# Linear-attention and gated-FFN kernel: the attention quotient between 32x32 block transpositions on VectorE instead of TensorE transposes

## Chip, cores and metric

The kernel runs on one core of one Trainium2 chip (trn2). The metric is the device time of one execution in microseconds; lower is better. Before the change it is 652.47 us, the median of 3 runs (651.65 to 653.05).

## What is computed

The input x has 16 batches of 512 tokens with 128 channels, fp32. Each batch goes through an attention block with eight heads of 16 channels and no softmax, and then through a gated FFN; both have a residual and a layer norm.

```python
normed = rms_norm(x, gamma)
q = taylor(normed @ w_q * 16 ** -0.5)        # [1, q, q x q * 0.5 ** 0.5]: 1 + 16 + 256 features
k = taylor(normed @ w_k); v = normed @ w_v
kv_state = sum_n k[n] v[n]; k_sum = sum_n k[n]
den = q . k_sum
att = (q . kv_state) / maximum(den, 1e-5)
x1 = layernorm(x + att @ w_out)
h = silu(x1 @ w1 * s1) * (x1 @ w2 * s2)      # 128 -> 512
h = gelu(h @ h1 * s); h = gelu(h @ h2 * s)   # 512 -> 512
out = layernorm(x1 + h @ w3 * s3)            # 512 -> 128
```

## The kernel before, in words

A batch passes four stages (FRONT, MIDDLE, FFN, TAIL), one per step, and four batches are in work at once: step t does the front of batch t, the middle of batch t-1, the FFN of batch t-2 and the tail of batch t-3. There are 19 steps; t = 3 to 15 have all four stages. Steps 0 to 2 and the last ones are written out, the others run in a loop. Every engine has its own `step` with its instructions in a fixed, handwritten order; semaphores join them. Nothing is reordered by a compiler, so an instruction that waits holds up everything behind it on its engine.

Numbers are split into a rounded part (hi) and the rest (lo). A product in the FFN is two matmuls of 512 columns, L421 with hi and L422 with lo.

PSUM has eight banks of 512 fp32 columns. Four form `ring` (attention), four `fps` (FFN). The tables `RING` and `FPS` list in TensorE's order what is written to which bank; `bank_wait` makes a write wait until the last content of its bank has been read. In the table before, bank n % 4 goes to the n-th entry.

The front: `transpose_x` and `project_kv` (L304, four token tiles), `project_q`, the sums of pairs of q (`sums_of_q`, sq0 to sq8, L330 to L334), which ScalarE squares into `phiT` (L619), the products of k on VectorE (L248, `phi_k_main`), and `state` (L337), the key/value state, which ScalarE copies to `st`.

The middle: `transpose_state`, `transpose_rest`, then `apply_main` and `apply_rest` (L369, L378) form numerator and denominator of all heads in two banks, acc0 and acc1. They lie channel by token: 32 partitions a head, of which 16 are the numerator and partition 17 (`DEN`) is the denominator. To divide, tokens must be on the partitions. So ScalarE copies both banks to `numden` (L683, L684), TensorE transposes them in eight pieces (`transpose_numden`, L387), VectorE takes maximum, reciprocal and product (`normalise`, L791, once per bank), TensorE transposes the result back in four pieces (`transpose_att`, L395), ScalarE copies it (L695), and `project_out` (L404) multiplies by w_out. `sum_x1` (L814), statistics and a scaling (L810) give x1, which is transposed for the FFN.

The FFN: layer1 (tiles a0, b0 to a3, b3; `silu` on ScalarE, `gate_mult`, `gate_hi`, `gate_lo` on VectorE), layer2 and layer3 (tiles two0 to two3, three0 to three3; two Gelu activations each on ScalarE, L657 and L658, then `gelu_tile` on VectorE, L876), layer4 (y, copied by `copy_y`, L663). layer3 works through hidden tiles 0, 1, 2 for three0 and three1, and each needs the L876 of its tile. The tail: `transpose_y`, `sum_z` (L830), statistics, scaling, store.

The DMA queue only loads x one step ahead, when the bank "out" of the step has been read, and stores the output.

In step 1 ScalarE also sums the low parts of all weights (`weights_lo_sum`, L636, three times), ahead of the first att copy. VectorE takes the largest of these sums (`largest_lo`, L951), TensorE transposes it (L520) and reads it into a register before step 2.

TensorE's order in a full step, with the parts that the change touches marked by a star: 

```
*transpose_state, *layer1(0), layer1(1), transpose_rest, transpose_x, layer1(2), apply_main,
layer1(3), kv0, apply_rest, transpose_y, kv1, layer2(0; 0-2), *transpose_numden x2,
layer2(1; 0-2), layer2(0; 3), layer2(1; 3), *transpose_att, kv2, layer2(2; 0-2), project_out,
project_q, layer2(2; 3), layer2(3), kv3, layer3(0; 0-2), layer3(1; 0-2), sq0, layer3(0; 3),
layer3(1; 3), sq1, sq8, layer3(2; 0-1), sq2, layer3(2; 2-3), sq3, layer3(3; 0-1), transpose_x1,
sq4, layer3(3; 2-3), layer4(0), sq5, layer4(1), *sq6, *state, layer4(2), sq7, layer4(3)
```

VectorE's order around the change (L897 to L928): gate_mult 3, gate_lo 2, gate_hi 3, gate_lo 3, phi_k_main 0, sum_z, normalise 0 and 1, phi_k_main 1, gelu_tile(0,0), the scaling of z, gelu_tile(0,1), sum_x1, gelu_tile(0,2), q_lo, gelu_tile(0,3).

Of the kernel before, what the change touches and what calls it, by code (L numbers as in the profile page):

```python
# [29 lines left out]
P = 128  # L30
# [12 lines left out]
RING = [(what, stage, n % 4) for n, (what, stage) in enumerate((  # L43
    ("stateT", MIDDLE), ("restT", MIDDLE), ("xT", FRONT), ("kv0", FRONT), ("acc0", MIDDLE),
    ("acc1", MIDDLE), ("kv1", FRONT),
    ("nt0", MIDDLE), ("nt1", MIDDLE), ("attT", MIDDLE), ("kv2", FRONT), ("out", MIDDLE), ("qT", FRONT), ("kv3", FRONT),
    ("sq0", FRONT), ("sq1", FRONT), ("sq8", FRONT), ("sq2", FRONT), ("sq3", FRONT), ("sq4", FRONT), ("sq5", FRONT),
    ("sq6", FRONT), ("state", FRONT), ("sq7", FRONT)))]
# [30 lines left out]
def build(nc, x, w_q, w_kv, w_out, w1t, w2t, h1t, h2t, w3t, scales, consts, sel_d, out):  # L79
# [9 lines left out]
    with ExitStack() as ctx:  # L89
# [59 lines left out]
        numden = wide[:, 0:2 * N].rearrange("p (g n) -> p g n", g=2)  # L149
        att_tok, yT = (wide[:, n * N:(n + 1) * N] for n in (2, 3))  # L150
        att = sb("att", [P, N])
        den = sb("den", [P, 2, NT, 4])
        rden = sb("rden", [P, 2, NT, 4])
# [44 lines left out]
        den_ready, rden_ready = sem("den_ready"), sem("rden_ready")  # L198
# [91 lines left out]
        def _(pe):  # L290
# [96 lines left out]
            def transpose_numden(t, g):  # L387
                pe.wait_ge(ring_free[bank_of(RING, f"acc{g}")], read(RING, t, f"acc{g}"))
                bank_wait(RING, ring_free, t, f"nt{g}")
                for j in range(NT):  # L390
                    mm = nc.tensor.transpose(ring[:, bank_of(RING, f"nt{g}"), j * P:(j + 1) * P],  # L391
                                             numden[:, g, j * P:(j + 1) * P], ident)
                mm.then_inc(ring_full, 1)

            def transpose_att(t):  # L395
                for g in range(2):
                    pe.wait_ge(ring_free[bank_of(RING, f"nt{g}")], read(RING, t, f"nt{g}"))
                bank_wait(RING, ring_free, t, "attT")
                for j in range(NT):
                    mm = nc.tensor.transpose(ring[:, bank_of(RING, "attT"), j * P:(j + 1) * P],  # L400
                                             att_tok[:, j * P:(j + 1) * P], ident)
                mm.then_inc(ring_full, 1)

            def project_out(t):  # L404
                pe.wait_ge(ring_free[bank_of(RING, "attT")], read(RING, t, "attT"))
# [62 lines left out]
            def steps_with(with_lo):  # L468
                def step(t, par, front, middle, ffn, tail):
                    if middle:  # L470
                        transpose_state(t)
                    if ffn:
                        layer1(t, 0, with_lo)
                        layer1(t, 1, with_lo)
# [20 lines left out]
                    if middle:  # L495
                        transpose_numden(t, 0)
                        transpose_numden(t, 1)
                    if ffn:
                        layer2(t, 1, (0, 1, 2), with_lo)
                        layer2(t, 0, (3,), with_lo)  # L500
                        layer2(t, 1, (3,), with_lo)
                    if middle:
                        transpose_att(t)
# [49 lines left out]
                    if front:  # L553
                        sums_of_q(t, 6)
                        state(t)
# [25 lines left out]
        def _(act):  # L581
# [84 lines left out]
            def step(t, par, front, middle, ffn, tail):  # L666
# [27 lines left out]
                if middle:  # L694
                    ring_copy(t, "attT", att[:, :], ring[:, bank_of(RING, "attT"), :])  # L695
# [403 lines left out]
```

## Time and profile before

| | |
|---|---|
| median of 3 runs | 652.47 us |
| profiled execution | 652.38 us |
| its span, first to last instruction | 650.6 us |
| TensorE matmul busy (PE) | 586.3 us, 90% |
| TensorE weight load busy (PEld) | 433.1 us, 67% |
| VectorE busy (DVE) | 470.1 us, 72% |
| ScalarE busy (ACT) | 467.5 us, 72% |
| GpSimd busy (POOL) | 147.8 us, 23% |
| mean granted TensorE clock | 0.976 |

The page gives busy time and waits by engine. Consecutive instructions overlap a little, so a busy sum can exceed the time that passes, and a start-to-start distance says more than a duration. A timeline gives each instruction's start; "idle before" in brackets says how long its engine had nothing to do and which instruction ended that. A line can be that of a helper: all ring copies on ScalarE show as L591.

### The profile page before, as it was taken

To read this page: it belongs to the slowest core of one execution; us is meant where nothing else is said; L and a number is where in the kernel's file an instruction comes from. 1 tells how busy PE (TensorE), PEld (TensorE's weight loads), DVE (VectorE), ACT (ScalarE), POOL (GpSimd) and SP (SyncE) were. 2 spreads that over 40 slices of the span, in tenths; PEclk is the share of its full clock that TensorE was granted. 3 is DMA by queue.
4 is the path that set the end of the run, shared out by engine and by line. 5 is a ranking of instruction groups with operands and counts; after the bars stand their busy time and mean duration, and the time that the engine had idled before them with its cause. 6 is when DMAs were issued, how large, how long until landed. Compare 5 with 4: busy or idle time off the path is not lost.

```text
span 650.6 us, 12112 instructions
## 1 busy us (share of the span) xinstructions
PE 586.3 (90%) x3921; PEld 433.1 (67%) x3921; DVE 470.1 (72%) x1069; ACT 467.5 (72%) x938; POOL 147.8 (23%) x216
## 2 busy tenths in 40 slices
PE   2554799999999999999999999999999999999994
PEld 1324577676858677676858677676858777686763
DVE  3466376977869686977959696986959696886673
ACT  2735569596877879686876969687786959686753
POOL 2551122122213122122113122121213122211000
PEclk9877899999999999999999999999999999999998
DMA  7000000000101010010000010000000000000000
GB/s 257 0 1 17 4 16 1 2 34 1 33 1 32 0 32 0 0 32 0 32 0 32 0 31 1 0 32 0 32 0 32 0 6 26 1 17 2 16 18 16
DMA packets 7367, 12.36 MB, mean 19 GB/s; under 512 B 816, under 2 KB 1840, under 8 KB 7344
## 3 DMA queue, kind: packets, MB, share of 16 engines
q1 hardware_dynamic: 7344, 12.06, 5.9%
q8 instruction: 14, 0.23, 0.2%
q14 instruction: 9, 0.07, 0.0%
HBM read 7.86 MB, written 4.19 MB: 19 GB/s over the span
## 4 chain that ended last, share of the span: by engine, by line
PE 59%; ACT 20%; issue 11%; DVE 3%; POOL 1%; ACTq 0%; POOLq 0%; DVEq 0%
PE fps L421 17%; PE fps L422 17%; ACT phiT L619 5%; ACT hid_hi L657 5%; PE ring L375 5%; PE ring L383 5%; PE ring L309 3%; PE ring L408 2%; ACT fps L658 2%; PE ring L391 2%; ACT restq L622 2%; ACT L641 2%; PE ring L316 1%; PE ring L400 1%; PE fps L464 1%
## 5 line engine op out<-in xcount | busy, mean ns | idle before, releaser
L421 PE MATMUL fps<-hid_hi,w_hi 128*128 128x512 f32 x576 | 229.7, 399 | 2.7 <-DVE hid_lo L876 1.4
L422 PE MATMUL fps<-hid_lo,w_hi 128*128 128x512 f32 x576 | 226.5, 393 | 0.0
L657 ACT ACTIVATE hid_hi<-fps,col 128x512 fp32r<-128x512 f32 x128 | 88.3, 690 | 64.2 <-PE fps L422 63.9
L421 PEld LDWEIGHTS fps<-hid_hi,w_hi 128*128 128x128 f32 x576 | 108.2, 188 | 29.9 <-issue 3.4
L876 DVE TENSOR_TENSOR hid_lo<-fps,hid_hi 128x512 fp32r<-128x512 f32 x128 | 88.1, 689 | 53.1 <-ACT fps L658 52.6
L422 PEld LDWEIGHTS fps<-hid_lo,w_hi 128*128 128x128 f32 x576 | 108.3, 188 | 20.9
L858 DVE SCALAR_TENSOR_TENSOR h<-fps,col,gate_zo 128x512 f32<-128x512 f32 x64 | 47.8, 747 | 75.7 <-ACT gate_zo L648 67.5
L619 ACT ACTIVATE phiT<-ring 128x512 f32<-128x512 f32 x128 | 73.6, 594 | 19.6 <-PE ring L330 19.5
L658 ACT ACTIVATE fps<-fps,col 128x512 f32<-128x512 f32 x128 | 84.5, 660 | 0.0
L248 DVE TENSOR_TENSOR phi_k<-phi_k 128x896 f32<-128x896 f32 x64 | 72.6, 1137 | 4.8 <-ACT v_one L591 4.3
L648 ACT ACTIVATE gate_zo<-fps,col 128x512 f32<-128x512 f32 x64 | 44.1, 689 | 40.2 <-PE fps L422 39.5
L1009 POOL TENSOR_TENSOR k_mid<-phi_k,v_one 128x256 f32<-128x256 f32 x32 | 21.4, 668 | 186.9 <-ACT v_one L591 151.2
L421 PE MATMUL fps<-x1T_hi,w_hi 128*128 128x512 f32 x128 | 55.7, 435 | 0.0
L330 PE MATMUL ring<-qT,sel 128*128 128x512 f32 x128 | 53.4, 429 | 1.0 <-DVE qT L779 0.7
L422 PE MATMUL fps<-x1T_lo,w_hi 128*128 128x512 f32 x128 | 51.2, 400 | 0.0
L868 DVE TENSOR_TENSOR hid_lo<-h,hid_hi 128x512 fp32r<-128x512 f32 x64 | 43.7, 683 | 0.5
L641 ACT ACT_TABLE_LOAD x33 | 42.3, 1283 | 1.3 <-PEq L1090 0.7
L347 PE MATMUL ring<-phi_k,v_one 128*32 128x153 f32 x1024 | 37.1, 296 | 4.5 <-ACT phiT L619 4.4
L1032 POOL TENSOR_TENSOR rstd<-veps,const 128x4 f32<-128x4 f32 x16 | 16.1, 1008 | 104.9 <-DVE veps L828 104.9
L347 PEld LDWEIGHTS ring<-phi_k,v_one 128*32 128x32 f32 x1024 | 31.3, 110 | 12.1 <-issue 9.0
L421 PEld LDWEIGHTS fps<-x1T_hi,w_hi 128*128 128x128 f32 x128 | 24.6, 192 | 17.5 <-issue 12.6
L990 POOL TENSOR_TENSOR rn<-ssc,const 128x4 f32<-128x4 f32 x16 | 16.3, 1021 | 80.7 <-DVE ssc L761 77.8
(111 smaller groups left out, 970.0 us busy)
## 6 DMA issues: line engine op xcount, KB each, us to landing
x_b<-in_x SPq DMA_DIRECT2D x16, 256.0 KB, 2.8
out<-gate_zo SPq DMA_DIRECT2D x16, 256.0 KB, 2.8
h<-in_h SPq DMA_DIRECT2D x1, 1024.0 KB, 8.3
gate_zo<-in_h SPq DMA_DIRECT2D x1, 1024.0 KB, 10.4
wide<-in_w SPq DMA_DIRECT2D x3, 256.0 KB, 4.5
sel_raw<-in_sel SPq DMA_DIRECT2D x1, 384.0 KB, 3.6
w_qkv_raw<-in_w_kv SPq DMA_DIRECT2D x1, 128.0 KB, 2.2
const<-in_consts SPq DMA_DIRECT2D x1, 115.0 KB, 2.3
```

The source lines that it names most:

```text
L248: return eng.tensor_tensor(out, fixed, moved, ALU.mult)
L330: mm = nc.tensor.matmul(ring[:, bank, :], sel[:, (f % 4) * P:(f % 4 + 1) * P], qT[f // 4][:, :], start=True, stop=True)
L347: mm = nc.tensor.matmul(ring[32 * hh:32 * hh + 32, bank, g * FEAT:(g + 1) * FEAT], v_one[:, j, 4 * g + hh, :], phi_k[:, j, 4 * g + hh, 0:F ...
L421: nc.tensor.matmul(fps[:, bank, :], w_hi[:, o:o + P], hi, start=start, stop=False)
L422: mm = nc.tensor.matmul(fps[:, bank, :], w_hi[:, o:o + P], lo, start=False, stop=stop and not with_lo)
L619: op = nc.scalar.activation(phiT[:, f, :], ring[:, bank, :], ACT.Square)
L641: nc.scalar.activation(table_use[:, :], source, function)
L648: nc.scalar.activation(gate[:, m % 2, :], fps[:, bank_of(FPS, f"a{m}"), :], ACT.Silu, scale=s1_c[:, m:m + 1]).then_inc(f_free[bank_of(FPS, ...
L657: nc.scalar.activation(hid[1 - layer][0][:, m, :], fps[:, bank, :], ACT.Gelu, scale=scale)
L658: nc.scalar.activation(fps[:, bank, :], fps[:, bank, :], ACT.Gelu, scale=scale)\
L858: nc.vector.scalar_tensor_tensor(out=h32[:, m, :], in0=fps[:, bank_of(FPS, b), :], scalar=s2_c[:, m:m + 1], in1=gate[:, m % 2, :], op0=ALU ...
L876: nc.vector.tensor_tensor(lo, fps[:, bank, :], hi.bitcast(F32), ALU.subtract)\
```

## The change

The denominator and numerator are no longer brought to token order by TensorE. VectorE's transposition works on each 32x32 block by itself: of a tile of 128 x 512 it transposes the 64 blocks in place. As a head occupies 32 partitions, one such operation out of PSUM puts, within every block, the tokens on the partitions and the 32 channels of a head on the columns. VectorE then takes the maximum, the reciprocal and the product for both banks at once, and a second block transposition turns the packed result back to channel by token. Its channel order differs from before (heads of both banks interleaved), so the rows of w_out are permuted on the host. The semaphore `att_ready` goes straight to `project_out`. The three ring entries nt0, nt1 and attT go, and the table gets new banks written out by hand.

With it come moves: on TensorE layer1(0) ahead of transpose_state and state ahead of sq6; on ScalarE sq3 ahead of x1_hi and the state copy ahead of sq6; on VectorE normalise ahead of sum_z.

```diff
@@ -40,12 +40,11 @@
-RING = [(what, stage, n % 4) for n, (what, stage) in enumerate((
-    ("stateT", MIDDLE), ("restT", MIDDLE), ("xT", FRONT), ("kv0", FRONT), ("acc0", MIDDLE),
-    ("acc1", MIDDLE), ("kv1", FRONT),
-    ("nt0", MIDDLE), ("nt1", MIDDLE), ("attT", MIDDLE), ("kv2", FRONT), ("out", MIDDLE), ("qT", FRONT), ("kv3", FRONT),
-    ("sq0", FRONT), ("sq1", FRONT), ("sq8", FRONT), ("sq2", FRONT), ("sq3", FRONT), ("sq4", FRONT), ("sq5", FRONT),
-    ("sq6", FRONT), ("state", FRONT), ("sq7", FRONT)))]
+RING = (
+    ("stateT", MIDDLE, 0), ("restT", MIDDLE, 1), ("xT", FRONT, 2), ("kv0", FRONT, 3), ("acc0", MIDDLE, 0),
+    ("acc1", MIDDLE, 1), ("kv1", FRONT, 2), ("kv2", FRONT, 3), ("out", MIDDLE, 0), ("qT", FRONT, 1), ("kv3", FRONT, 2),
+    ("sq0", FRONT, 3), ("sq1", FRONT, 0), ("sq8", FRONT, 2), ("sq2", FRONT, 1), ("sq3", FRONT, 3), ("sq4", FRONT, 0),
+    ("sq5", FRONT, 2), ("state", FRONT, 1), ("sq6", FRONT, 3), ("sq7", FRONT, 2))
...
-        numden = wide[:, 0:2 * N].rearrange("p (g n) -> p g n", g=2)
+        num_tok = wide[:, 0:2 * N]
...
@@ -384,25 +384,8 @@
-            def transpose_numden(t, g):
...
-            def transpose_att(t):
...
             def project_out(t):
-                pe.wait_ge(ring_free[bank_of(RING, "attT")], read(RING, t, "attT"))
+                pe.wait_ge(att_ready, t)
                 bank_wait(RING, ring_free, t, "out")
@@ -467,10 +450,11 @@
+                    if ffn:
+                        layer1(t, 0, with_lo)
                     if middle:
                         transpose_state(t)
                     if ffn:
-                        layer1(t, 0, with_lo)
                         layer1(t, 1, with_lo)
@@ -492,15 +476,9 @@
                     if ffn:
                         layer2(t, 0, (0, 1, 2), with_lo)
-                    if middle:
-                        transpose_numden(t, 0)
-                        transpose_numden(t, 1)
-                    if ffn:
                         layer2(t, 1, (0, 1, 2), with_lo)
                         layer2(t, 0, (3,), with_lo)
                         layer2(t, 1, (3,), with_lo)
-                    if middle:
-                        transpose_att(t)
@@ -551,8 +529,8 @@
                     if front:
+                        state(t)
                         sums_of_q(t, 6)
-                        state(t)
@@ -679,9 +657,6 @@
-                if middle:
-                    ring_copy(t, "acc0", numden[:, 0, :], ring[:, bank_of(RING, "acc0"), :])
-                    ring_copy(t, "acc1", numden[:, 1, :], ring[:, bank_of(RING, "acc1"), :])
@@ -691,8 +666,6 @@
-                if middle:
-                    ring_copy(t, "attT", att[:, :], ring[:, bank_of(RING, "attT"), :])
@@ -718,10 +691,12 @@
+                if front:
+                    square_sums(t, 3)
                 if middle:
                     x1_hi(t)
                 if front:
-                    square_sums(t, 3, 4)
+                    square_sums(t, 4)
@@ -729,10 +704,9 @@
-                    square_sums(t, 6)
                     ring_copy(t, "state", st[:, :, :].rearrange("p g f -> p (g f)"),
                               ring[:, bank_of(RING, "state"), 0:2 * FEAT])
-                    square_sums(t, 7)
+                    square_sums(t, 6, 7)
@@ -788,20 +762,24 @@
-            def normalise(t, g):
...
+            def normalise(t):
+
+                for g in range(2):
+                    bank = bank_of(RING, f"acc{g}")
+                    dve.wait_ge(ring_full, written(RING, t, f"acc{g}"))
+                    nc.vector.transpose(num_tok[:, g * N:(g + 1) * N], ring[:, bank, :]).then_inc(ring_free[bank], 1)
+                num = num_tok.rearrange("p (g b e) -> p g b e", g=2, e=32)
+                for g in range(2):
+                    dve.wait_ge(ring_free[bank_of(RING, f"acc{g}")], read(RING, t, f"acc{g}"))
+                nc.vector.tensor_scalar(den[:, :, :], num[:, :, :, DEN], DEN_EPS, None, ALU.max).then_inc(den_ready, 1)
+                dve.wait_ge(den_ready, t)
+                nc.vector.reciprocal(rden[:, :, :], den[:, :, :]).then_inc(rden_ready, 1)
+                dve.wait_ge(rden_ready, t)
+                nc.vector.tensor_tensor(att_tok.rearrange("p (b g e) -> p g b e", g=2, e=DH), num[:, :, :, 0:DH],
+                                        rden[:, :, :].unsqueeze(3).to_broadcast([P, 2, N // 32, DH]), ALU.mult)\
+                    .then_inc(att_tok_ready, 1)
+                dve.wait_ge(att_tok_ready, t)
+                nc.vector.transpose(att[:, :], att_tok).then_inc(att_ready, 1)
@@ -901,13 +879,12 @@
                     phi_k_main(t, 0)
-                if tail:
-                    sum_z(t, 1 - par)
                 if middle:
                     if is_step(t, 1):
                         dve.wait_ge(w_lo_ready[0], 1)
-                    normalise(t, 0)
-                    normalise(t, 1)
+                    normalise(t)
+                if tail:
+                    sum_z(t, 1 - par)
@@ -1067,6 +1044,7 @@
+    data["w_out"] = _np.ascontiguousarray(data["w_out"].reshape(2, 4, DH, 128).transpose(1, 0, 2, 3).reshape(128, 128))
```

## Rows read from the trace of the kernel before

**Rows 1.** The page: busy time of the engines and TensorE's granted clock in 40 slices
```profile
PE 586.3 (90%) x3921; PEld 433.1 (67%) x3921; DVE 470.1 (72%) x1069; ACT 467.5 (72%) x938; POOL 147.8 (23%) x216
...
PEclk9877899999999999999999999999999999999998
```

**Rows 2.** Busy by window, one step: length, PE, PEld, DVE, ACT, POOL, clock, DMA
```profile
331.67:368.52 36.85, 35.75 (x245) 26.65 (x246) 28.63 (x66) 28.50 (x59) 8.53 (x14) 1.00 0.04 14
```

**Rows 3.** The same view, two stretches of that step
```profile
339.02:352.82 13.80, 13.72 (x84) 10.44 (x78) 12.98 (x39) 9.09 (x22) 3.61 (x5) 1.00 0.07 19
356.55:369.45 12.90, 11.88 (x108) 9.29 (x107) 7.31 (x13) 12.83 (x24) 3.21 (x6) 1.00 0.00 0
```

**Rows 4.** Timeline of PE: start us, us, engine, line, operation, [idle before <-releaser]
```profile
353.78 0.39 PE L421 MATMUL fps<-hid_hi,w_hi 128*128 128x512 f32 x1
...
368.52 0.43 PE L357 MATMUL ring<-const,st 128*128 128x128 f32 x2 [0.67 <-ACT st L591]
...
369.75 0.39 PE L421 MATMUL fps<-x1T_hi,w_hi 128*128 128x512 f32 x1
```

**Rows 5.** Timeline of DVE in the same step
```profile
342.35 0.68 DVE L835 TENSOR_TENSOR gate_zo<-x,fps 128x512 f32<-128x512 f32 x1
...
344.54 0.17 DVE L796 TENSOR_SCALAR den<-ring 128x16 f32<-128x16 f32 x1
344.74 0.25 DVE L799 RECIPROCAL rden<-den 128x16 f32<-128x16 f32 x1
...
346.20 1.08 DVE L248 TENSOR_TENSOR phi_k<-phi_k 128x896 f32<-128x896 f32 x1
347.20 0.68 DVE L876 TENSOR_TENSOR hid_lo<-fps,hid_hi 128x512 fp32r<-128x512 f32 x1
347.80 1.11 DVE L810 TENSOR_SCALAR gate_zo<-gate_zo,zmv,zrstd 128x128 f32<-128x128 f32 x4
...
349.70 0.69 DVE L817 TENSOR_TENSOR x1p<-x_b,ring 128x512 f32<-128x512 f32 x1 [0.19 <-PE ring L408]
...
352.13 0.69 DVE L876 TENSOR_TENSOR hid_lo<-fps,hid_hi 128x512 fp32r<-128x512 f32 x1 [0.18 <-ACT fps L658]
```

**Rows 6.** Timeline of ACT, end of the same step
```profile
368.75 0.70 ACT L663 ACTIVATE wide<-fps,col 128x512 f32<-128x512 f32 x1
```

**Rows 7.** Timeline of PE around the transposes that the change removes
```profile
342.98 1.04 PE L391 MATMUL ring<-const,wide 128*128 128x128 f32 x8
343.77 0.47 PE L421 MATMUL fps<-hid_hi,w_hi 128*128 128x512 f32 x1
...
345.92 0.39 PE L422 MATMUL fps<-hid_lo,w_hi 128*128 128x512 f32 x1
...
346.77 0.37 PE L309 MATMUL ring<-w_qkv_hi,xnT_hi 128*128 128x264 f32 x1
```

**Rows 8.** Groups by line: line, engine, operation, xcount | busy us, mean ns | idle before
```profile
L876 DVE TENSOR_TENSOR hid_lo<-fps,hid_hi 128x512 fp32r<-128x512 f32 x128 | 88.1, 689 | 53.1 <-ACT fps L658 52.6
...
L864 DVE CAST hid_hi<-h 128x512 fp32r<-128x512 f32 x64 | 26.9, 420 | 0.6
...
L802 DVE TENSOR_TENSOR wide<-ring,rden 128x256 f32<-128x256 f32 x32 | 13.6, 424 | 1.1
```

**Rows 9.** Waits: engine line <- releaser: us in total, times, longest
```profile
PE ring L347 <- ACT phiT L619: 4.4, 13, 0.4
```

**Rows 10.** Timelines of ACT, PE and DVE in step t = 1
```profile
52.36 0.58 ACT L591 ACTIVATE att<-ring 128x512 f32<-128x512 f32 x1
...
61.46 0.37 PE L520 MATMUL fps<-const,lo_max 128*1 128x128 f32 x1 [4.90 <-DVE lo_max L954]
...
55.10 0.69 DVE L817 TENSOR_TENSOR x1p<-x_b,ring 128x512 f32<-128x512 f32 x1 [5.41 <-PE ring L408]
...
57.38 0.68 DVE L779 TENSOR_TENSOR qT<-ring,qT 64x512 fp32r<-64x512 f32 x1
```

More of the change, by code:

```diff
@@ L148, in build @@
         wide = sb("wide", [P, 4 * N])
-        numden = wide[:, 0:2 * N].rearrange("p (g n) -> p g n", g=2)
+        num_tok = wide[:, 0:2 * N]
         att_tok, yT = (wide[:, n * N:(n + 1) * N] for n in (2, 3))
         att = sb("att", [P, N])
-        den = sb("den", [P, 2, NT, 4])
-        rden = sb("rden", [P, 2, NT, 4])
+        den = sb("den", [P, 2, N // 32])
+        rden = sb("rden", [P, 2, N // 32])
         x1p = sb("x1p", [P, NT, D])
@@ L197, in build @@
         st_rest_ready = sem("st_rest_ready")
-        den_ready, rden_ready = sem("den_ready"), sem("rden_ready")
+        den_ready, rden_ready, att_tok_ready, att_ready = (
+            sem(n) for n in ("den_ready", "rden_ready", "att_tok_ready", "att_ready"))
         mv_ready, veps_ready, rstd_ready, x1_ready = (
@@ L385, in apply_rest @@
                     mm.then_inc(ring_full, 1)
-            def transpose_numden(t, g):
[L388 to L393, printed above, removed]
-            def transpose_att(t):
[L396 to L402, printed above, removed]
             def project_out(t):
-                pe.wait_ge(ring_free[bank_of(RING, "attT")], read(RING, t, "attT"))
+                pe.wait_ge(att_ready, t)
                 bank_wait(RING, ring_free, t, "out")
@@ L789, in q_linear @@
                 nc.vector.tensor_copy(restq[1][64:P, :], ring[64:P, bank, :]).then_inc(ring_free[bank], 1)
-            def normalise(t, g):
-                bank = bank_of(RING, f"nt{g}")
-                nt = ring[:, bank, :].rearrange("p (j h e) -> p j h e", j=NT, h=4)
-                dve.wait_ge(ring_full, written(RING, t, f"nt{g}"))
-                nc.vector.tensor_scalar(den[:, g, :, :], nt[:, :, :, DEN], DEN_EPS, None, ALU.max)\
-                    .then_inc(den_ready, 1)
-                dve.wait_ge(den_ready, 2 * (t - 1) + g + 1)
-                nc.vector.reciprocal(rden[:, g, :, :], den[:, g, :, :]).then_inc(rden_ready, 1)
-                dve.wait_ge(rden_ready, 2 * (t - 1) + g + 1)
-                out = att_tok.rearrange("p (j h e) -> p j h e", j=NT, h=H)[:, :, 4 * g:4 * g + 4, :]
-                nc.vector.tensor_tensor(out, nt[:, :, :, 0:DH],
-                                        rden[:, g, :, :].unsqueeze(3).to_broadcast([P, NT, 4, DH]), ALU.mult)\
-                    .then_inc(ring_free[bank], 1)
+            def normalise(t):
[15 more added lines that the diff above has]
+                nc.vector.transpose(att[:, :], att_tok).then_inc(att_ready, 1)
             def norm_scale(n, sm, mv2, rs, s_mv, s_rs, dst, ready):
```

## The prediction

> **What bounds the kernel now.** I read first the page's busy rows: TensorE is busy 90% of the span at a granted clock of 1.00 (2.4 GHz) in most slices (9 stands for 0.9 or more; it is lower in slices 2 to 5) [rows 1], so an operation taken off it looks like time won. The second view, busy time by window, gives the repeating step: 36.85 us, PE busy 35.75, VectorE 28.63, ScalarE 28.50 [rows 2]. Shares hide where each engine binds, so I went to the timelines. Two more windows of the same view, [rows 3], are the finding: from 339.02 to 352.82 VectorE works 12.98 of 13.80 us, and from 356.55 to 369.45 ScalarE works 12.83 of 12.90. Each has a long stretch with practically no slack, and TensorE, which feeds both and waits on both, closes the loop.
>
> The loop, in the step shown: layer1's a1 (PE, 332.90, one period before the 369.75 of [rows 4]) leads to a3, to silu 3 and to gate_mult 3 (VectorE, 339.02). VectorE runs its queue in order from there to gelu_tile(0,2) at 352.13 [rows 5]. TensorE takes that result in layer3 (its matmul at 353.78 [rows 4]). Then three0 fills, ScalarE starts its solid stretch at 356.55 and ends it with copy_y (368.75 plus 0.70 [rows 6]); y's bank frees a1.
>
> **What goes from TensorE.** Eight numden transposes: the first starts at 342.98, the next product at 343.77, so 0.79 us. Four att transposes: the product ahead starts at 345.92 and needs 0.23, the projection behind starts at 346.77, so 0.62 us, a short wait included. The matmul behind each block has 0.47 and 0.37 us instead of 0.39 and 0.28, 0.08 more each. Sum 1.57 us a step [rows 7]. On ScalarE three copies of 128x512 go, 1.8 us; they lie where it waits for TensorE (its solid stretch begins at 356.55), so I count them at nothing in the repeating step.
>
> **What comes onto VectorE.** Removed: two groups of maximum, reciprocal, multiply, 344.54 to 346.20, so 1.66 us [rows 5]. Added: two transpositions out of PSUM, one maximum, one reciprocal, a multiply of 512 columns, a transposition within SBUF. No row shows a block transposition. Below it I put the cast of 128x512 in SBUF, 0.42 us; above it four 128-column instructions in place of one, 1.11 us [rows 5, 8]. The nearest rows are 512 fp32 columns read from PSUM, 0.689 us [rows 8], and I take 0.69 for all three. Starts of neighbours that do not depend on each other are 0.08 closer than their durations (347.20 plus 0.68, next start 347.80), those behind a semaphore 0.03 apart. So: 0.61 + 0.72 + 0.20 (maximum) + 0.37 (reciprocal: 0.25, 0.08 for twice the columns, and the gap; the 0.08 is what 16 columns cost more here than in the maximum) + 0.72 (multiply, 256 columns take 0.42, 512 in the other rows 0.69) + 0.61 = 3.23 us. Net 1.57 us more for VectorE, within its solid stretch.
>
> The Trainium skill, "VectorE: DVE Perf Modes", section "The three transpose paths", gives a 128x128 bf16 transposition as 311 ns on VectorE and 390 on TensorE, and its "Rules for kernel authors" send a 128x128 transposition to TensorE. No row here tests the 311; with one element a cycle, as "Vector Engine (DVE) Microarchitecture Reference", section 3.8, has it, an estimate for 512 columns is 0.71 us, which would put the total 0.9 us higher. The rule argues against this change, and VectorE's full stretch says why it may be right here.
>
> **Does VectorE hold TensorE back?** The stretch has two waits left, before sum_x1 (349.70, shown as 0.19) and before gelu_tile(0,2) (352.13, shown as 0.18); with the 0.08 by which starts could overlap that is 0.27 + 0.26 us [rows 5]. With att ready at about 345.6 and project_out due at 347.0, TensorE does not wait there. But gelu_tile(0,2) now starts at 352.13 + 1.57 - 0.53 = 353.17 and ends at 353.86, while TensorE, 1.57 earlier, wants it at 352.21. So the matmul at 353.78 moves to 353.91: instead of 1.57 us won, 0.13 lost, and TensorE stands 1.7 us at layer3's third tile (L421), waiting for L876. **The removed TensorE time is turned into a wait on VectorE.**
>
> **Moves and their cover.** layer1(0) goes ahead of transpose_state. Today TensorE waits 0.67 us there for the state copy, 0.85 counting from the spacing of two matmuls [rows 4]. In its place a1 waits for copy_y, whose time is set by ScalarE's solid stretch, in which the same instructions are only reordered. It ends at 369.45; a1 starts 0.13 behind it (as the transposes do behind the state copy), 369.58 instead of 369.75: 0.17 won. state before sq6, and its bank freed by sq2 instead of sq3, removes a wait of 0.35 (4.4 us in 13 waits [rows 9]), but a1 waits for ScalarE all the same, so that is worth nothing. three3 now waits about 0.3 us for its bank (gelu_tile(1,0) starts near 359.5 instead of 358.9); the 1.2 us that just came free cover that. sq7's bank waits for sq5 instead of sq4, ended 366.1, wanted at 366.8. normalise ahead of sum_z delays sum_z by about 3.2 us; behind it are the yT bank, wanted by two3 at 349.1, freed at 346.2; the POOL power and the output's store, which nothing waits for; and phi_k_main(1). The load of x waits for sum_x1, about a microsecond later, and has most of a step. The permuted w_out is made on the host: nothing.
>
> **Sum.** A repeating step changes by 0.13 - 0.17 = -0.04 us; 13 of them (t = 3 to 15) give -0.5. In t = 2 there is no sum_z (342.35 to 344.54, 2.19 us [rows 5]) and no final scale, so VectorE is early and TensorE keeps its gain: -1.57 - 0.17 = -1.7. In t = 16, without front work, the same count gives +0.15.
>
> The first attention step (t = 1) is another matter. There the att copy stands in ScalarE's queue behind the three sums over the weights' low parts and starts at 52.36; project_out follows, then sum_x1 at 55.10, and at 61.46 TensorE waits 4.90 us for lo_max, which VectorE reaches behind all that [rows 10]. Without the copy att is ready at about 48.7 and sum_x1 starts near 50.9. q_lo must then wait for the q copies, which are still behind those sums: 53.1 plus 0.6, so 53.75 instead of 57.38, 3.65 us earlier; the chain behind moves with it. At the end of this step state and sq7 come about 0.4 earlier, and a0 is not behind the state transposes, 0.24. Together -4.3.
>
> -0.5 - 1.7 + 0.15 - 4.3 = -6.4 us. The profiled execution took 652.38 us (span 650.6 and 1.8 around it), the median of the runs is 652.47: forecast **646.0 us**. Each 0.1 us on the price of a transposition is 0.3 a step and, over 14 steps, 4.2 us.
>
> **Rivals.**
> (A) The forecast: both loops bind, 641 to 651 us. Chance 0.66.
> (B) Slower: a transposition costs more than other 512-column instructions, with its place in VectorE's stretch before gelu_tile(0,2). It decides from 6.4 / (3 x 14) = 0.15 over my price, 0.84 us each; at the upper bound of 1.11 it is +17.6, 663.6 us. For it: no row shows the instruction. Against: everything simple with 512 columns out of PSUM takes 0.67 to 0.69. Chance 0.16, a third of it near zero change.
> (C) TensorE stays the bound and the whole gain comes: 15 x (1.57 + 0.17) + 4.3 = 30.4, so 622 us. For it: 90% busy. Against: VectorE's stretch would have to end 1.6 us sooner than its queue adds up to. Chance 0.08.
> (D) The first step's gain does not come, because something else holds lo_max (the third sum ends only at about 52.4, and largest_lo waits for it): 650.3 us. Against: the wait names VectorE, and 57.8 is well behind 52.4. Chance 0.10.
> If the last transposition alone ran at the cast's 0.42 it would be 14 x 0.27 = 3.8 less, 642.2, within (A).
>
> **Numbers.** (A) with its bounds is 641 to 651; down to 638 takes cheap transpositions with a little more slack, up to 655 takes in (D) and (B) to 0.9 us each. Outside are most of (C) and half of (B). A difference of 0.2%, 1.3 us, is what a measurement can tell. Faster: nearly all of (A), (C), half of (D): 0.74. Same: 0.13. Slower: 0.13.
>
> **What would show it.** A period near 36.8 us; PE waits at L421 for L876 (about 1.7 us a step) and for copy_y (0.8), together nearly as large as the time removed; no wait at L357 or L347; VectorE solid from gate_mult 3 to gelu_tile(0,2) with transpositions of 0.69; lo_max's transpose at about 57.8. Wrong if the period is near 35.1 (then C), or over 37.2 with transpositions over 0.84 (B).

## The result, and the profile after

The changed kernel takes 679.58 us (median of 4 runs, 678.40 to 681.73) against 652.06 us for the kernel before beside it: a ratio of 1.042 (95% interval 1.039 to 1.045). It is **slower by 27.5 us**, where 6.4 less was forecast.

The page after, where it answers to [rows 1]: busy times, and TensorE's granted clock in 40 slices.
```profile
span 678.1 us, 11624 instructions
...
PE 588.8 (87%) x3729; PEld 427.5 (63%) x3729; DVE 500.6 (74%) x1069; ACT 440.0 (65%) x890; POOL 158.6 (23%) x216
...
PEclk9876999899998989899898989989898998989898
```
192 TensorE instructions are gone and yet its busy time is 2.5 us longer; the second row says why: in about every second slice the clock is below 9 tenths, where before it was so only in slices 2 to 5 and in the last.

The waits of PE after (releaser: us in total, times, longest):
```profile
PE fps L404 <- DVE hid_lo L854: 34.1, 30, 2.1
...
PE fps L404 <- ACT wide L641: 9.3, 14, 0.9
```
L404 and L405 are the hi and lo products (L421 and L422 before), L854 is gelu_tile (L876), L641 copy_y. These are the two waits that the prediction named, in the places it named; the first is longer.

**Closing the loop.** I cut one period of the prediction's loop at five events and read each from the timelines. After, two kinds of period alternate.

| stretch | before | as predicted | after |
|---|---|---|---|
| gate_mult 3 to gelu_tile(0,2) | 13.11 | 14.15 | 15.18 / 15.21 |
| to TensorE's third tile | 1.65 | 0.74 | 0.74 / 0.74 |
| to ScalarE's gelu(1,0) | 2.77 | 2.77 | 4.01 / 4.31 |
| to the end of copy_y | 12.90 | 12.90 | 12.92 / 12.92 |
| to the next gate_mult 3 | 6.38 | 6.21 | 6.24 / 6.26 |
| period | 36.81 | 36.77 | 39.09 / 39.44 |

Three stretches came out as predicted to within 0.05 us. Two did not: the first is 1.05 too long, the third 1.24 or 1.54. Over the whole trace, counted from transpose_x1 to transpose_x1, the period is 39.28 us in the mean of 13 steps against 36.83.

*The first stretch.* VectorE's timeline, then POOL's, in the step that begins at 346.65 (start us, us, engine, line, [idle before]):
```profile
346.65 0.75 DVE L836 SCALAR_TENSOR_TENSOR h<-fps,col,gate_zo 128x512 f32<-128x512 f32 x1 [0.63 <-ACT gate_zo L626]
...
349.98 1.31 DVE L770 STREAM_TRANSPOSE wide<-ring 128x512 f32<-128x512 f32 x2
351.33 0.70 DVE L774 TENSOR_SCALAR den<-wide 128x32 f32<-128x32 f32 x1
352.06 0.35 DVE L776 RECIPROCAL rden<-den 128x32 f32<-128x32 f32 x1
352.45 0.69 DVE L778 TENSOR_TENSOR wide<-wide,rden 128x512 f32<-128x512 f32 x1
353.17 0.71 DVE L782 STREAM_TRANSPOSE att<-wide 128x512 f32<-128x512 f32 x1
...
355.96 1.09 DVE L248 TENSOR_TENSOR phi_k<-phi_k 128x896 f32<-128x896 f32 x1
356.97 0.69 DVE L854 TENSOR_TENSOR hid_lo<-fps,hid_hi 128x512 fp32r<-128x512 f32 x1
358.06 1.11 DVE L788 TENSOR_SCALAR gate_zo<-gate_zo,zmv,zrstd 128x128 f32<-128x128 f32 x4 [0.40 <-POOL zrstd L1009]
...
361.86 0.69 DVE L854 TENSOR_TENSOR hid_lo<-fps,hid_hi 128x512 fp32r<-128x512 f32 x1
```
```profile
351.22 0.76 POOL L990 TENSOR_TENSOR phi_k<-phi_k,k_mid 128x256 f32<-128x256 f32 x1
356.10 1.82 POOL L1009 TENSOR_TENSOR zrstd<-zveps,const 128x4 f32<-128x4 f32 x1 [4.12 <-DVE zveps L824]
```
The transpositions, the multiply and the reciprocal cost what was taken for them. The maximum of 32 columns does not: it takes 0.70 where 0.20 was taken, and it stands beside GpSimd's L990, ending 0.05 behind it. And the power for zrstd takes 1.82, where the kernel before has 1.01 for it; it starts 0.14 behind L248 on VectorE, a product of two SBUF inputs. The scaling of z (L788) has to wait for it: 0.40 shown, 0.48 by the start it would have had at 0.08 before the end of the L854 ahead. Together 0.53 + 0.48 = 1.01 of the 1.05.

*The third stretch.* TensorE's timeline behind the wait, in that step and then in the one before it:
```profile
359.82 0.50 PE L404 MATMUL fps<-hid_hi,w_hi 128*128 128x512 f32 x1 [0.33 <-DVE hid_lo L854]
...
362.60 0.79 PE L404 MATMUL fps<-hid_hi,w_hi 128*128 128x512 f32 x1 [2.04 <-DVE hid_lo L854]
363.19 0.63 PE L405 MATMUL fps<-hid_lo,w_hi 128*128 128x512 f32 x1
363.62 0.63 PE L404 MATMUL fps<-hid_hi,w_hi 128*128 128x512 f32 x1
...
365.75 0.40 PE L405 MATMUL fps<-hid_lo,w_hi 128*128 128x512 f32 x1
365.99 0.39 PE L330 MATMUL ring<-qT,sel 128*128 128x512 f32 x1
```
```profile
323.48 0.50 PE L404 MATMUL fps<-hid_hi,w_hi 128*128 128x512 f32 x1 [2.05 <-DVE hid_lo L854]
...
324.74 0.58 PE L405 MATMUL fps<-hid_lo,w_hi 128*128 128x512 f32 x1
325.11 0.63 PE L404 MATMUL fps<-hid_hi,w_hi 128*128 128x512 f32 x1
```
Matmuls that start every 0.23 us elsewhere start every 0.43 here: the lower of the two clock levels, 1.2 GHz instead of 2.4. Busy by window says the same (length, PE, PEld, DVE, ACT, POOL, clock):
```profile
358.80:367.00 8.20, 5.83 (x19) 4.06 (x19) 7.92 (x20) 2.74 (x8) 2.80 (x4) 0.79 0.22 64
```
In one kind of period the slow matmuls begin right behind the wait of 2.04 us, in the other 1.3 us later; that is the alternation of 39.4 and 39.1. The wait is twice paid: once as the wait, and once as the speed of what was held up.

**The rest of the span.** transpose_x1 of step 1 starts at 58.80 instead of 64.26. Of these 5.46 us, 1.56 are there when kv0 of step 1 starts (41.59, 43.15 before), and 3.9 come behind it. Of the 1.56, 0.36 lie before TensorE's first matmul (9.86, 10.22 before); the other 1.2 come in steps 0 and 1. One part of them is in step 0, where the kernel before waits for the bank of kv2, and the changed kernel, with its new bank table, doesn't:
```profile
15.13 0.59 PE L309 MATMUL ring<-w_qkv_hi,xnT_hi 128*128 128x264 f32 x1 [0.66 <-ACT v_one L591]
```
How the rest of the 1.2 divides over banks, order and clock is not shown. The next period is 1.34 shorter, but seven matmuls of it ran at the lower clock before and one after, which is most of that. Then 13 periods are 2.45 longer each, the last 2.50: -5.46 - 1.34 + 31.85 + 2.50 = 27.55, the difference of the two spans (678.1 - 650.6) to 0.05.

### The profile page after: what moved, and what is told of

Its sections match the earlier page's. It is cut to its first block, busy times and chain, and to the rows that moved or that the text cites. A ratio compares the mean times of both kernels' runs of the same rounds, so it can differ in the third digit from the quotient of the medians.

```text
span 678.1 us, 11624 instructions
## 1 busy us (share of the span) xinstructions
PE 588.8 (87%) x3729; PEld 427.5 (63%) x3729; DVE 500.6 (74%) x1069; ACT 440.0 (65%) x890; POOL 158.6 (23%) x216
## 4 chain that ended last, share of the span: by engine, by line
PE 29%; DVE 24%; ACT 19%; issue 16%; POOL 5%; DVEq 1%; ACTq 0%; POOLq 0%
PE fps L404 10%; PE fps L405 8%; ACT phiT L597 5%; PE ring L375 5%; POOL zrstd L1009 4%; ACT fps L636 3%; ACT hid_hi L635 3%; DVE hid_lo L854 3%; DVE wide L770 3%; DVE phi_k L248 2%; DVE gate_zo L788 2%; PE ring L330 2%; ACT gate_zo L626 2%; ACT wide L641 2%; DVE zstats L818 2%
## 5 line engine op out<-in xcount | busy, mean ns | idle before, releaser
L404 PE MATMUL fps<-hid_hi,w_hi 128*128 128x512 f32 x576 | 241.7, 420 | 35.4 <-DVE hid_lo L854 34.1
L405 PE MATMUL fps<-hid_lo,w_hi 128*128 128x512 f32 x576 | 238.0, 413 | 0.0
L404 PEld LDWEIGHTS fps<-hid_hi,w_hi 128*128 128x128 f32 x576 | 114.6, 199 | 71.5 <-DVE hid_lo L854 47.4
L405 PEld LDWEIGHTS fps<-hid_lo,w_hi 128*128 128x128 f32 x576 | 115.5, 201 | 23.9
L854 DVE TENSOR_TENSOR hid_lo<-fps,hid_hi 128x512 fp32r<-128x512 f32 x128 | 88.0, 689 | 52.1 <-ACT fps L636 51.1
L248 DVE TENSOR_TENSOR phi_k<-phi_k 128x896 f32<-128x896 f32 x64 | 70.6, 1105 | 5.6 <-ACT v_one L569 5.1
L404 PE MATMUL fps<-x1T_hi,w_hi 128*128 128x512 f32 x128 | 55.2, 432 | 13.7 <-ACT wide L641 9.3
L330 PE MATMUL ring<-qT,sel 128*128 128x512 f32 x128 | 55.9, 448 | 1.9 <-DVE qT L753 0.7
L1009 POOL TENSOR_TENSOR zrstd<-zveps,const 128x4 f32<-128x4 f32 x16 | 26.6, 1663 | 105.8 <-DVE zveps L824 105.8
L569 ACT ACTIVATE phi_k<-ring 128x128 f32<-128x128 f32 (+1 forms) x128 | 24.9, 257 | 39.6 <-PE ring L309 38.5
L405 PE MATMUL fps<-x1T_lo,w_hi 128*128 128x512 f32 x128 | 50.4, 393 | 0.0
L404 PEld LDWEIGHTS fps<-x1T_hi,w_hi 128*128 128x128 f32 x128 | 24.0, 187 | 34.7 <-issue 17.8
L347 PE MATMUL ring<-phi_k,v_one 128*32 128x153 f32 x1024 | 37.2, 298 | 0.0
```

Source lines behind the costliest of these rows:

```text
L248: return eng.tensor_tensor(out, fixed, moved, ALU.mult)
L330: mm = nc.tensor.matmul(ring[:, bank, :], sel[:, (f % 4) * P:(f % 4 + 1) * P], qT[f // 4][:, :], start=True, stop=True)
L404: nc.tensor.matmul(fps[:, bank, :], w_hi[:, o:o + P], hi, start=start, stop=False)
L405: mm = nc.tensor.matmul(fps[:, bank, :], w_hi[:, o:o + P], lo, start=False, stop=stop and not with_lo)
L854: nc.vector.tensor_tensor(lo, fps[:, bank, :], hi.bitcast(F32), ALU.subtract)\
L1009: nc.gpsimd.tensor_tensor(rs[:, :], var[:, :], neg_half[:, :], ALU.pow).then_inc(rs_ready, 1)
```

## The experiments

Three things are suspected, and all would follow from VectorE's queue: the maximum beside GpSimd, the power beside L248, and the clock behind the wait. The rival is that the transposition as such costs too much there. Ratios are to the kernel before on the same chip, with the 95% interval.

**1. Fill the wait, and change nothing else.** Eight more matmuls (`fill`, four products of hi and lo into the bank of three1 before it is wanted) stand between layer3's second and third tile in the full steps.
```diff
-                        layer3(t, 0, (0, 1, 2), with_lo)
+                        layer3(t, 0, (0, 1), with_lo)
+                        if middle and tail:
+                            fill(t, 4, with_lo)
+                        layer3(t, 0, (2,), with_lo)
                         layer3(t, 1, (0, 1, 2), with_lo)
```


> The changed kernel; TensorE repeats one product (8 matmuls of 512 columns, 1.85 us, result overwritten later) in the wait of 2.04 us before layer3's third tile, in the steps with all of middle and tail. Theory (three added costs: the maximum waits for GpSimd, 0.5 us; GpSimd's power is slowed and the scaling of z waits for it, 0.5 us; and TensorE's clock halves behind the 2 us wait, 1.3 us a step): the matmuls behind the wait come every 0.23 us again, not every 0.43, the period falls from 38.97 to about 37.7 and the total from 678 to about 661 us. Rival (the halved clock is hidden behind the wait for the next VectorE result, gelu_tile(0,3), and the loop is VectorE's alone): the clock comes back and the total stays at 677 to 680 us.

661.76 us, 1.013 (1.009 to 1.016), as expected. Periods of 38.04 in the mean, and behind step 2 not one slow matmul (PE, the third tile):
```profile
353.95 0.50 PE L404 MATMUL fps<-hid_hi,w_hi 128*128 128x512 f32 x1 [0.20 <-DVE hid_lo L862]
354.28 0.39 PE L405 MATMUL fps<-hid_lo,w_hi 128*128 128x512 f32 x1
```
**More work on TensorE makes the kernel 18 us faster**: of 39.28 us a period, 1.24 are the clock's, and nothing else was touched.

**2. Take GpSimd away from the maximum.** `k_small(0)` goes behind both powers in POOL's queue.
```diff
-                if front:
-                    k_small(t, 0)
 ...
                     inv_std(t - 1, veps_ready, veps, rstd, rstd_ready)
+                if front:
+                    k_small(t, 0)
```


> The changed kernel with GpSimd's small products of token tiles 0 and 1 (L986 to L990) moved behind its two powers, away from the quotient on VectorE. Theory: the maximum (L774) falls from 0.68 to about 0.2 us in every step, VectorE reaches gelu_tile(0,2) 0.5 us sooner, period 38.5, total about 671 us. Rival (reading 32 columns at a stride of 32 from SBUF is what makes the maximum slow): it stays at 0.68 and so does the total, 678 us. Either way the power of zrstd keeps its 1.8 us.

659.00 us, 1.010 (1.007 to 1.013), 12 better than expected. The maximum takes 0.19:
```profile
L774 DVE TENSOR_SCALAR den<-wide 128x32 f32<-128x32 f32 x16 | 3.1, 192 | 0.8
```
The price of the maximum was right; what came on top is the clock. The wait is as long as before, and what is behind it is not slow (PE):
```profile
351.87 0.40 PE L405 MATMUL fps<-hid_lo,w_hi 128*128 128x512 f32 x1
354.30 0.50 PE L404 MATMUL fps<-hid_hi,w_hi 128*128 128x512 f32 x1 [2.04 <-DVE hid_lo L854]
354.64 0.39 PE L405 MATMUL fps<-hid_lo,w_hi 128*128 128x512 f32 x1
```
So the length of this one wait does not decide it: at 2.04 us the clock falls in every period of the changed kernel and in only one here, where a period is 37.55, 38.04 (experiment 1) less the 0.5. The stretches around it are not equal, though: the changed kernel also waits 0.33 at the tile before (359.82 above), which is gone here, also in the one period that falls.

**3. Give TensorE other work during the wait.**
```diff
-                        layer3(t, 0, (0, 1, 2), with_lo)
-                        layer3(t, 1, (0, 1, 2), with_lo)
+                        layer3(t, 0, (0, 1), with_lo)
+                        layer3(t, 1, (0, 1), with_lo)
+                        layer3(t, 0, (2,), with_lo)
+                        layer3(t, 1, (2,), with_lo)
```


> The changed kernel; on TensorE layer3(1) of tiles 0 and 1 stands ahead of layer3(0) of tile 2, so that 4 useful matmuls (0.93 us) fall into the wait. Theory: the wait shrinks from 2.04 to about 1.1 us and three0 is full when gelu_tile(0,3) allows it, 1.0 to 1.3 us sooner; period 37.7 to 38.0, total 661 to 665 us, a little more if the clock still halves. Rival (VectorE's loop alone): 677 to 680 us.

663.92 us, 1.016 (1.008 to 1.024), as expected; the interval is wide, since its two executions are 4 us apart. The wait is now 1.13 and 0.75 us, the period 38.0 with two of 39.4, in which seven and eight matmuls are slow. Work brought forward keeps the clock like the filler in all but these two, and shortens nothing else: VectorE sets the time.

**4. Take VectorE work out of the stretch: sum_x1 behind gelu_tile(0,3).**
```diff
-                if middle:
-                    sum_x1(t, 1 - par)
                 if ffn:
                     gelu_tile(t, 0, 2)
 ...
                     gelu_tile(t, 0, 3)
+                if middle:
+                    sum_x1(t, 1 - par)
```


> The changed kernel with sum_x1 and its statistics (2.2 us of VectorE) moved behind gelu_tile(0,3), out of the stretch that TensorE waits for. Theory (VectorE's queue before gelu_tile(0,2) is the bound): gelu_tile(0,2) starts 2.2 us sooner, the wait on TensorE all but goes, the clock stays at 1.00, and the next bound is ScalarE's stretch before copy_y: period about 35.5, total 630 to 640 us, faster than both kernels. Rival (the bank that sum_x1 frees is then late for sq1): a new wait of 1 to 2 us at sq1, period 37, total 650 to 655 us.

674.35 us, 1.032 (1.029 to 1.035): a miss by 34 and more. The wait comes back one result later (PE):
```profile
334.00 0.51 PE L404 MATMUL fps<-hid_hi,w_hi 128*128 128x512 f32 x1 [2.08 <-DVE hid_lo L854]
```
Here it is three3 that waits for its bank, which gelu_tile(1,0) frees. VectorE is full beyond gelu_tile(0,2), up to gelu_tile(1,0), and what leaves the first part only goes to the second. (The scaling of x1 was also slower now, 1.72 instead of 1.11, beside GpSimd.) Most periods are 38.0; in three of the thirteen, of 39.5 to 39.8, six to eight matmuls behind this wait are slow. Another 8 us of the miss lie in steps 1 and 2, where transpose_x1 comes 4.2 and then 7.8 us later than in the changed kernel.

**5. As 2, with the scaling of z behind gelu_tile(0,3).** This takes away the wait for the power too.
```diff
-                if tail:
-                    norm_scale(t - 3, z, zmv, zrstd, ...)
 ...
                     gelu_tile(t, 0, 3)
+                if tail:
+                    norm_scale(t - 3, z, zmv, zrstd, ...)
```


> Run e2 (GpSimd's small products moved away) and also the scaling of z moved behind gelu_tile(0,3) on VectorE, so that nothing waits for the slowed power of zrstd and 1.5 us leave the stretch before gelu_tile(0,2). Theory, corrected by e4 (VectorE is in work without a gap from gate_mult 3 to gelu_tile(1,0), and taking work out of its first part only moves TensorE's wait to three3's bank): the wait at layer3's third tile falls from 2.0 to 0.6 us, that at layer3(3) grows from 0.5 to about 1.5; the period gains only the 0.4 us of the removed wait, 37.1, total about 651 us. Rival (only the stretch before gelu_tile(0,2) counts): period 36.0, total about 637 us.

651.20 us, 0.998 (0.997 to 1.000), as expected: period 37.26, no slow matmuls behind step 2, VectorE's wait for zrstd gone. But TensorE still waits 0.62, 0.64 and 1.22 us, and the scaling pays for its new neighbour on GpSimd with 2.21 us instead of 1.11:
```profile
351.85 2.21 DVE L788 TENSOR_SCALAR gate_zo<-gate_zo,zmv,zrstd 128x128 f32<-128x128 f32 x4
```

**6. Relieve VectorE.** As 2, scaling of z behind gelu_tile(0,2); the q copies (1.4 us, `q_linear`) and gate_hi 3 go to ScalarE, the copies behind `copy_q`.
```diff
 (VectorE)
-                    q_linear(t)
-                    gate_hi(t, 3)
 (ScalarE)
                     copy_kv(t, 0)
+                if ffn:
+                    act.wait_ge(f_free[bank_of(FPS, "b3")], read(FPS, t, "b3"))
+                    nc.scalar.activation(hid[0][0][:, 3, :], h32[:, 3, :], ACT.Copy).then_inc(hi_ready, 1)
 ...
                     copy_q(t)
+                    q_linear(t)
```


> e5's idea with less work on VectorE: the scaling of z right behind gelu_tile(0,2), the two copies of q for the linear features (1.4 us) and the cast gate_hi 3 (0.45 us) given to ScalarE, in its idle time. Theory: gelu_tile(1,0) starts 2.2 us sooner than in e2 (37.55 us a period), so that TensorE and ScalarE bound again: period 35.4 to 36.0, clock at 1.00 throughout, total 632 to 641 us, faster than both kernels. Rival (ScalarE, given 1.8 us more, becomes the bound): period 36.8 or more, total over 650 us.

656.16 us, 1.005 (1.004 to 1.007): a miss by 15 and more. 1.8 us less on VectorE, of which the scaling of z, 1.71 instead of 1.11 beside GpSimd, takes back 0.6, and the period is 37.4: TensorE now waits for ScalarE as well (sq0 for q, 0.29; gelu_tile(0,3) behind its activation, 0.87; a1 for copy_y, 0.84). ScalarE is no reserve at this place, and period and total are those of the rival.

**7. The change without its quotient.** The kernel before, with the moves on TensorE and ScalarE only; sum_z stays ahead of normalise, and the bank table is the old one with state and sq6 exchanged.
```diff
-                    if middle:
-                        transpose_state(t)
                     if ffn:
                         layer1(t, 0, with_lo)
+                    if middle:
+                        transpose_state(t)
 ...
-                        sums_of_q(t, 6)
                         state(t)
+                        sums_of_q(t, 6)
```
(and on ScalarE the copy of the state ahead of the squares of 6, the squares of 3 ahead of x1_hi)

> The kernel before with the moves on TensorE and ScalarE alone: layer1(0) ahead of transpose_state, state ahead of sq6 with the bank of sq2, sq3 ahead of x1_hi, state copy ahead of sq6; the quotient as before. Theory: the waits at L357 and L347 (13.6 us in all) go, but ScalarE's stretch before copy_y sets the pace, so only 0.1 to 0.2 us a step are won: total 649 to 651 us. Rival (those waits were time): 13 us less, 639 us.

649.79 us, 0.996 (0.995 to 0.997). Period 36.69 (36.83 before), the waits at L357 and L347 gone, a1 waiting for copy_y (11.9 us in 14). These moves are worth 0.14 us a period (0.17 was taken).

**8. Undo one reordering: sum_z ahead of normalise, as it was.**
```diff
+                if tail:
+                    sum_z(t, 1 - par)
                 if middle:
                     if is_step(t, 1):
                         dve.wait_ge(w_lo_ready[0], 1)
                     normalise(t)
-                if tail:
-                    sum_z(t, 1 - par)
```


> The changed kernel with sum_z ahead of normalise on VectorE, as it was before. Theory: the maximum meets no GpSimd products (0.2 us), the power of zrstd takes 1.0 us and its result is there in time, so 1.0 us leaves VectorE's stretch; att is ready 2 us later and project_out waits about 0.9 us, but that only takes from the wait behind it; the clock falls seldom or never. Period 37.5 to 38.0, total 657 to 663 us. Rival (the quotient has to come first, since project_out holds up all of layer3): 678 us or more.

649.28 us, 0.995 (0.993 to 0.997), 8 better than the lower end of what was expected. **The order of two entries in VectorE's queue is 30 us**, and the period is 37.03, with no slow matmul behind step 2. VectorE and POOL of this kernel:
```profile
339.36 1.31 DVE L770 STREAM_TRANSPOSE wide<-ring 128x512 f32<-128x512 f32 x2
340.71 0.19 DVE L774 TENSOR_SCALAR den<-wide 128x32 f32<-128x32 f32 x1
```
```profile
338.42 0.75 POOL L990 TENSOR_TENSOR phi_k<-phi_k,k_mid 128x256 f32<-128x256 f32 x1
339.50 1.01 POOL L1009 TENSOR_TENSOR zrstd<-zveps,const 128x4 f32<-128x4 f32 x1 [0.33 <-DVE zveps L824]
```
L990 is over when the maximum starts, and the power runs beside the transpositions out of PSUM at its full speed. The three block transpositions themselves are unchanged, so the rival that they are too dear here falls. The waits that are left:
```profile
PE ring L391 <- DVE att L782: 14.4, 15, 2.4
...
PE fps L404 <- DVE hid_lo L854: 8.8, 16, 0.7
PE fps L404 <- ACT wide L641: 8.6, 13, 0.9
```
project_out waits 0.83 a step for att, since the quotient now stands behind sum_z. The repeating step wins nothing by all this: 37.03 us against 36.83 in the kernel before. What is won against that kernel lies in steps 0 and 1: transpose_x1 of step 1 starts at 57.99 instead of 64.26.

**9 and 10. Use VectorE's slack where it is, behind gelu_tile(1,0).** Both are experiment 2 with phi_k_main and the scaling of z moved late. In 9 (norm_scale also leaves its place behind gelu_tile(0,0)):
```diff
                     q_linear(t)
-                    phi_k_main(t, 2)
 ...
                     gelu_tile(t, 1, 0)
                 if front:
-                    phi_k_main(t, 3)
+                    phi_k_main(t, 2)
                 if ffn:
                     gelu_tile(t, 1, 1)
+                if front:
+                    phi_k_main(t, 3)
+                if tail:
+                    norm_scale(t - 3, z, zmv, zrstd, ...)
```
and in 10, where phi_k_main(t, 2) and norm_scale leave their old places as in 9:
```diff
-                if front:
-                    phi_k_main(t, 1)
                 if ffn:
                     gelu_tile(t, 0, 0)
 ...
                     gelu_tile(t, 1, 0)
+                if front:
+                    phi_k_main(t, 1)
+                if ffn:
+                    gelu_tile(t, 1, 1)
+                if front:
+                    phi_k_main(t, 2)
+                    phi_k_main(t, 3)
 ...
                     gelu_tile(t, 1, 2)
+                if tail:
+                    norm_scale(t - 3, z, zmv, zrstd, ...)
```


> Run e5 with more of VectorE's work moved behind what TensorE waits for: phi_k_main(2) behind gelu_tile(1,0), phi_k_main(3) and the scaling of z behind gelu_tile(1,1). Theory (the changed kernel is bound by the order of VectorE's queue from gate_mult 3 to gelu_tile(1,0)): gelu_tile(1,0) starts 3.3 us sooner than in e5, where the scaling of z also met GpSimd (2.2 instead of 1.1 us); the waits at three3's bank (1.2) and at sq2 (0.6) go, that at layer3's third tile (0.6) stays; period 35.4 to 36.0, total 629 to 637 us. Rival (state then waits for phi_k_main(3), or ScalarE's stretch is the bound): a new wait at L347 or L404 behind L641, period 36.6 to 37.2, total 643 to 651.

> As e9, with phi_k_main(1) moved as well, behind gelu_tile(1,0); 2 and 3 behind gelu_tile(1,1), the scaling of z behind gelu_tile(1,2). Nothing that reads two SBUF operands then runs beside the power of zrstd. Theory: that power takes 1.0 us instead of 1.8, gelu_tile(0,2) starts 1.0 us sooner than in e9 and the wait at layer3's third tile goes; period 35.0 to 35.6 (ScalarE's stretch), total 624 to 632 us. Rival: state waits for phi_k_main(3), a wait of over 1 us at L347, total no better than e9's.

633.16 us, 0.971 (0.969 to 0.973), period 36.04; and **621.02 us, 0.952 (0.950 to 0.954)**, period 35.05. The first is in the range expected, the second a little better. One period of the second by window, and its waits:
```profile
305.65:340.70 35.05, 34.56 (x235) 25.38 (x234) 30.99 (x67) 26.70 (x56) 8.60 (x13) 1.00 0.05 15
```
```profile
PE fps L404 <- DVE hid_lo L854: 6.9, 15, 0.7
...
PE fps L404 <- ACT wide L641: 2.8, 9, 0.9
```
TensorE is busy 34.56 of 35.05 us at full clock: it is the bound, where ScalarE's stretch was expected to be. The wait at layer3's third tile is gone; the 6.9 us for L854 are 0.4 a step at the last matmuls of layer4, which need gelu_tile(1,3). The scaling of z stands ahead of that on VectorE and takes 1.92 beside GpSimd.

**11. As 8, with the scaling of z behind gelu_tile(1,1).**
```diff
-                if tail:
-                    norm_scale(t - 3, z, zmv, zrstd, ...)
 ...
                     gelu_tile(t, 1, 1)
+                if tail:
+                    norm_scale(t - 3, z, zmv, zrstd, ...)
```


> Run e8 (sum_z ahead of the quotient) with the scaling of z moved behind gelu_tile(1,1). Theory: project_out's wait for att (0.83 us) stays, the wait at layer3's third tile (0.52) goes; period 36.4 to 36.6, total 641 to 644 us. Rival (ScalarE's stretch is all): 649 us as e8.

637.92 us, 0.978 (0.975 to 0.981), 3 better than expected, period 36.17, with 0.84 for att and 0.81 for copy_y left.

**12. The control: the orders of 10 and the moves of 7, with the old quotient on TensorE.** One order is not that of 10: sum_z stands ahead of normalise, as before.


> The control for e10: the quotient as in the kernel before (TensorE transposes, ScalarE copies), with the moves of e7 and with e10's orders on VectorE and GpSimd. Theory: without the removal TensorE is the bound and VectorE's order is worth next to nothing; period 36.6 to 36.7, total 648 to 650 us, as e7, so that e10's gain over it, some 28 us, is that of the block transpositions. Rival (e10's gain is that of the new orders): under 635 us.

649.63 us, 0.995 (0.993 to 0.997), period 36.70, no better than the moves alone. TensorE still waits for copy_y:
```profile
PE fps L421 <- ACT wide L664: 11.4, 14, 0.9
```
So the 28.6 us between this kernel and 10 belong to the block transpositions, with the bank table that goes with them: about 1.63 us a period, and 6 us in steps 0 and 1. Before, VectorE's slack was of no use, since TensorE and ScalarE bound; with the quotient on VectorE it is worth all that TensorE gives up.

## Why the prediction was wrong

**What held.** The finding that the transposes' time on TensorE turns into a wait at layer3's third tile is right: 2.04 us stand where 1.7 was forecast, and the third tile starts 0.74 behind gelu_tile(0,2), as it was worked out. The transposition costs 0.691 us out of PSUM and 0.712 within SBUF (0.69 taken), the reciprocal 0.353 and the multiply 0.692. a1 waits 0.4 to 0.9 us for copy_y (0.8), the waits at L357 and L347 are gone, and the moves alone gave 0.14 us a period for 0.17. Step 1 gave 3.9 for 4.3 (lo_max's transpose at 56.00, which without the 1.56 us that lie before kv0 is 57.56, for 57.8); the 1.2 that came ahead of that, behind the first matmul, stand in no term of the sum. t = 2 gave 1.34 for 1.7, which is luck: seven matmuls at the lower clock before and one after make most of it. Rival D is out, and so is B: its mechanism needs transpositions over 0.84 us. The time fell on B's side all the same, with another cause.

The estimate of 0.71 us for 512 columns, worked out from the 311 ns in "VectorE: DVE Perf Modes", "The three transpose paths", and one element a cycle in "Vector Engine (DVE) Microarchitecture Reference", section 3.8, of the Trainium skill, agrees with 0.691 and 0.712. The rule of the Trainium skill in "VectorE: DVE Perf Modes", "Rules for kernel authors", sends a full 128x128 transposition to TensorE and calls VectorE's the fastest for 32x32 blocks. So it does not argue against this change, as the prediction has it, for the change works on 32x32 blocks. Experiment 10 against 12, 28.6 us, agrees with the row on blocks once VectorE's queue is in order.

**What failed**, step by step, per period:

- *"0.20 (maximum)"*, in the sum of what comes onto VectorE. 0.70 measured, 0.53 in starts. The row behind it [rows 5] is a maximum that reads PSUM, beside no GpSimd work that mattered; the new one reads SBUF beside L990. Experiment 2 returns it to 0.19 and 8 to 0.205 by moving one or the other.
- *"normalise ahead of sum_z delays sum_z by about 3.2 us; behind it are ... the POOL power and the output's store, which nothing waits for"*. This is the step that broke most, since undoing it in experiment 8 removes the other two costs as well. The scaling of z, in VectorE's stretch, does wait for that power; and the delay put the power beside phi_k_main 1 (1.82 instead of 1.01). Its own cost is 0.48 us.
- *The wait as a plain wait.* The sum priced the wait at its length and the work behind it at the clock of before. It costs 1.24 or 1.54 us more where the clock falls; experiment 1 gives 1.24 by itself, 18 us of 679.58. No term of the sum and no bound of the range had it.

0.53 + 0.48 + 1.4 (the mean of 1.24 and 1.54) = 2.4, against 2.45 - (-0.04) = 2.49 measured over the forecast. Experiment 8, which undoes the second step alone, comes to 649.28: inside the range, 3.3 above the forecast. The forecast was thus nearly right for the change without that one swap, and the swap alone carried all three failures, the clock too. That closeness is partly luck: the period of experiment 8 is 0.26 longer than forecast, 3.4 us in 13, with project_out waiting 0.83 for att. The time of rival C, 622 us, is what experiment 10 reached with TensorE as the bound.

What is open: why the clock falls behind a wait of 2.04 us in one kernel and hardly ever behind an equal one in another. The changed kernel waits a further 0.33 just before and experiment 2 does not, but its one fall came without that wait too, and no run changes it alone. The runs show that both happen, not what decides.

## What to carry to other kernels

When work moves onto an engine with a full stretch, price each instruction with its new neighbours and its new source (PSUM or SBUF), and list who waits for every result that a reordering delays, GpSimd's included. A wait of TensorE can cost its length and then the clock on top; if a wait can't be avoided, work put into it, even useless work, may pay. And before judging such a trade, move what has no due time out of the full stretch into the slack: here that turned +4.2% into -4.8%.

## What the runs showed of the hardware

- **VectorE instructions on SBUF beside GpSimd.** Maximum of 32 columns 0.19 to 0.70; scaling of z or x1 (4 x 128 columns) 1.11 to 1.72 (experiment 4), 1.92 (10) and 2.21 (5). The other way round, GpSimd's power of four columns goes from 1.01 to 1.82 beside L248, which reads two tensors from SBUF. Transpositions out of PSUM beside the same power were not slowed, and the power neither (experiment 8). The maximum ends 0.05 behind L990, as if held until then. "SBUF — State Buffer" of the Trainium skill, section "SBUF: two separate sides", says that a VectorE instruction in a 2-port mode, or one with two SBUF inputs beside a GpSimd instruction that reads SBUF, and GpSimd's instruction exclude each other: the one that starts first has the shared port pair for its whole length. The power agrees with it: it starts 0.14 behind L248, which reads two SBUF inputs, and ends 0.87 behind L248's end, less than the 1.01 that it takes alone. In which mode the maximum or the scaling runs no run here shows.
- **The clock after a wait.** In the changed kernel 7 or 8 matmuls per period run at the lower clock, behind 2.04 us of waiting. With the same wait in experiment 2 it happened in one period, and with the wait filled in none. In experiment 3 it happened twice in thirteen periods, behind waits of 1.13 and 0.75, and in experiment 4 three times, behind a wait of 2.08.
- **Block transposition.** 128x512 fp32 in 0.691 us from PSUM, 0.712 from SBUF, as dear as VectorE's other instructions with 512 columns out of PSUM (0.689 for gelu_tile).
